# Attention's two ends reordered in a fused graph network kernel: V's products, VectorE's head sums, and Wo before the last centring

## The chip, the cores and the metric

One core of one Trainium2 chip. The metric is the device time of one execution in microseconds (us), the median of several runs. The kernel before took 464.77 us (three runs, 464.75 to 464.81).

## What is computed

The kernel fuses four graph-network layers on 512 nodes with 512 features, fp32. Only the first is touched, and in it only the attention. The softmax runs over axis 1 of scores with shape (node, head, other node), that is over the **heads**, not over the nodes:

```
q = (x @ Wq + bq).reshape(N, H, HEAD)        # N = 512, H = 8, HEAD = 64
k = (x @ Wk + bk).reshape(N, H, HEAD)
v = (x @ Wv + bv).reshape(N, H, HEAD)
scores = einsum('nhd,mhd->nhm', q, k) / sqrt(HEAD)
scores = where(adj[:, None, :] == 0, -1e9, scores)
attn = softmax(scores, axis=1)               # over the 8 heads
attn_out = einsum('nhm,mhd->nhd', attn, v).reshape(N, D) @ Wo + bo
h1 = layer_norm(x + attn_out, g1, be1)
ff = relu(h1 @ W1 + b1) @ W2 + b2
return layer_norm(h1 + ff, g2, be2)
```

The three later layers (a mean over edges, four experts over edges, a normalised graph convolution) follow one another and each needs the whole result of the one before.

## The kernel before, in words

**Engines and order.** Each engine has its own instruction list, written out by hand, and waits on semaphores; nothing is reordered at run time. TensorE is PE in the profile, VectorE DVE, ScalarE ACT, GpSimd POOL, and SyncE (SP) issues most DMAs.

**Tiling of the attention.** It runs in `STEPS = 8` steps. Step i takes a tile of 128 of the other nodes (m, `mt = i % 4`) and one half, 256, of the query nodes (`half = i // 4`), for all 8 heads. In each step:

- `scores(i, g)` for g = 0 and 1, four heads each: two bf16 matmuls that write the mask (L1415) and four score products (L1419, in the trace eight passes). The groups rotate through three pairs of PSUM banks, so a group from the third on waits until ACT has exponentiated the group two before it (`exp_done`).
- `coarse_scores(i, g)` on ACT copies the group's scores to bf16 (L655); a copy waits on `max_read`, VectorE's reading of the step before. `maxima(i)` on VectorE is the maximum over heads in three instructions (L923 or L928, L930, L933), the last of which writes `m_bf`.
- `centre(i, g)` on PE subtracts that maximum from the scores by two matmuls (L1426).
- `exponentials(i)` on ACT, two activations (L641), one a group.
- The sum over heads: GpSimd adds pairs of heads in two instructions (L537, `pair_sum`), then VectorE reduces these (L951, `head_sum`), except in step 0, where VectorE does it with four additions of its own (L943 to L948). `head_inverse` is a reciprocal (L957), and `normalised(i)` scales the exponentials (L399).
- `values(i, part_no)` on PE multiplies the probabilities by V (L1441, eight passes for four heads), and adds into banks 0 and 1. After steps 3 and 7 ACT copies these out (`attended_out`, L646), and `att_made` lets PE begin `values(4, 0)` and the Wo products.

**V.** V's tiles are four accumulating products each (L1331, two passes each in the trace), which PE works off in pieces (`values_part(t, *steps)`) between the scores of the first steps; VectorE adds the bias row (`values_in(t)`, L911). V products wait for all four tiles.

**After the steps** come the Wo tiles (`plain_rows_tile`, L1331), each followed on VectorE by residual, layer norm statistics and normalisation (`h1_start`, `h1_finish`), then transposes (L1282) and W1 (from L1509).

**GpSimd's other work nearby:** the last quarter of W1's low half (L490, waiting on `sums_made`), two DMAs that add rows to x_sb and h_sb, and the power for each layer norm (L505). SP's next weight load waits for that L490.

**VectorE's order around the change** (before):

```
head_sum(0); maxima(1); values_in(2); head_inverse(0); normalised(0)
maxima(2); head_sum(1); values_in(3); head_inverse(1)
for i in 2..7: maxima(i + 1); normalised(i - 1); head_sum(i); head_inverse(i)
```

Of the kernel before, what the change touches and what calls it, by code (L numbers as in the profile page):

```python
# [39 lines left out]
def build(nc, d, out):  # L40
    N, D = d["x"].shape
    E = d["src"].shape[0]
    NT = N // P
# [9 lines left out]
    STEPS = 2 * NT  # L53
# [196 lines left out]
    with ctx:  # L250
# [214 lines left out]
        def _(gp):  # L465
# [56 lines left out]
            gp.wait_ge(total_ask, 1)  # L522
            for k in range(DT - 1):
                split_lo_tile(W1A, k)
            gp.wait_ge(sums_made, 1)
            split_lo_tile(W1A, DT - 1)
            gp.wait_ge(ln_out, ln_out_no(LN0, NT - 1))
            add_row("L0_gnn_be2", x_sb, be2_added)
            gp.wait_ge(tr_done, tr_no(T0, NT - 1))
            add_row("L0_gnn_bo", h_sb, bo_added)  # L530
            for i in range(1, STEPS):

                e, pairs = e_bufs[i % E_BUFS], pair_sums[i % 2]
                gp.wait_ge(sums_made, max(i - 1, 1))
                for g in range(2):
                    gp.wait_ge(exp_done, 2 * i + g + 1)
                    gp.tensor_tensor(pairs[:, :, 2 * g:2 * g + 2].rearrange("p n h -> p h n"), e[:, 4 * g:4 * g + 2],  # L537
                                     e[:, 4 * g + 2:4 * g + 4], ALU.add).then_inc(pairs_made, 1)
# [26 lines left out]
        def _(act):  # L565
# [78 lines left out]
            def attended_out(half):  # L644
                act.wait_ge(pv_done, 2 * NT * (half + 1))
                nc.scalar.activation(att_sb[:, :, half * HN:(half + 1) * HN], attended(), ACT.Copy)\  # L646
                  .then_inc(att_made, 1)

            def coarse_scores(i, g):

                act.wait_ge(score_done, 2 * i + g + 1)
                if i >= 1:
                    act.wait_ge(max_read, i)
                heads = s_bf[:, g * HEADS // 2:(g + 1) * HEADS // 2]
                nc.scalar.activation(heads.rearrange("p (w b) n -> p w b n", w=2), group_scores(i, g), ACT.Copy)\  # L655
                  .then_inc(coarse_made, 1)

            coarse_scores(0, 0)
            for i in range(STEPS):
                exponentials(i)  # L660
                if i == 0:
                    coarse_scores(1, 0)
                if DIRECT <= i + 1 < STEPS:
                    coarse_scores(i + 1, 1)
                if i == NT + 2:
                    attended_out(0)
                if i + 2 < STEPS:
                    coarse_scores(i + 2, 0)
            attended_out(1)
# [90 lines left out]
        def _(v):  # L760
# [148 lines left out]
            def values_in(t):  # L909
                v.wait_ge(v_done, t + 1)  # L910
                nc.vector.tensor_tensor(v_sb[:, t, :], ps[:, v_bank(t), :], bv_row[:], ALU.add).then_inc(v_made, 1)  # L911
# [5 lines left out]
            def maxima(i):  # L917
                if i >= 1:
                    v.wait_ge(max_done, i)
                if i < DIRECT:  # L920
                    v.wait_ge(coarse_made, i + 1)
                    v.wait_ge(score_done, 2 * (i + 1))
                    nc.vector.tensor_tensor(s_max[:].rearrange("p (w b) n -> p w b n", w=2),  # L923
                                            s_bf[:, 0:4].rearrange("p (w b) n -> p w b n", w=2), group_scores(i, 1),
                                            ALU.max).then_inc(max_read, 1)
                else:
                    v.wait_ge(coarse_made, 2 * i)
                    nc.vector.tensor_tensor(s_max[:], s_bf[:, 0:4], s_bf[:, 4:8], ALU.max).then_inc(max_read, 1)  # L928
                v.wait_ge(max_read, i + 1)
                link(nc.vector.tensor_tensor(s_max[:, 0:2], s_max[:, 0:2], s_max[:, 2:4], ALU.max))  # L930
                if i >= 1:
                    v.wait_ge(centred, 2 * i)
                nc.vector.tensor_tensor(m_bf[:], s_max[:, 0], s_max[:, 1], ALU.max).then_inc(max_done, 1)  # L933
# [4 lines left out]
            def head_sum(i):  # L938

                e, r = e_bufs[i % E_BUFS], rsum[:, i % 2, :]  # L940
                if i == 0:
                    v.wait_ge(exp_done, 1)
                    nc.vector.tensor_tensor(half_sum[:, 0:2], e[:, 0:2], e[:, 2:4], ALU.add).then_inc(first_half, 1)  # L943
                    v.wait_ge(exp_done, 2)
                    link(nc.vector.tensor_tensor(half_sum[:, 2:4], e[:, 4:6], e[:, 6:8], ALU.add))
                    v.wait_ge(first_half, 1)
                    link(nc.vector.tensor_tensor(half_sum[:, 0:2], half_sum[:, 0:2], half_sum[:, 2:4], ALU.add))
                    nc.vector.tensor_tensor(r, half_sum[:, 0], half_sum[:, 1], ALU.add).then_inc(sums_made, 1)  # L948
                else:
                    v.wait_ge(pairs_made, 2 * i)  # L950
                    nc.vector.tensor_reduce(r, pair_sums[i % 2][:], AX_X, ALU.add).then_inc(sums_made, 1)  # L951

            def head_inverse(i):

                r = rsum[:, i % 2, :]
                v.wait_ge(sums_made, i + 1)
                nc.vector.reciprocal(r, r).then_inc(rinv_made, 1)  # L957

            def normalised(i):

                v.wait_ge(rinv_made, i + 1)
                if i < STEPS - 1:
                    probabilities(nc.vector, i, slice(0, HEADS)).then_inc(prob_done, 2)
                else:
                    probabilities(nc.vector, i, slice(0, HEADS // 2)).then_inc(prob_done, 1)
                    probabilities(nc.vector, i, slice(HEADS // 2, HEADS)).then_inc(prob_done, 1)

            head_sum(0)
            maxima(1)
            values_in(2)  # L970
            head_inverse(0)
            normalised(0)
            maxima(2)
            head_sum(1)
            values_in(3)
            head_inverse(1)
            for i in range(2, STEPS):
                if i + 1 < STEPS:
                    maxima(i + 1)
                normalised(i - 1)  # L980
                head_sum(i)
                head_inverse(i)
# [283 lines left out]
        def _(pe):  # L1266
# [61 lines left out]
            def plain_rows_tile(bank, t, src, w, done, steps=(0, 1, 2, 3)):  # L1328

                for k in steps:  # L1330
                    last = nc.tensor.matmul(ps[:, bank, :], src[:, k, col(t)], w[:, k, :], start=k == 0,  # L1331
                                            stop=k == DT - 1)
                if k == DT - 1:
                    last.then_inc(done, 1)

            def values_part(t, *steps):
                plain_rows_tile(v_bank(t), t, T_sb, w_v, v_done, steps)
# [92 lines left out]
            def values(i, part_no):  # L1430

                mt = i % NT
                if i == 0:
                    pe.wait_ge(v_made, NT)
                if i == NT:
                    pe.wait_ge(att_made, 1)
                pe.wait_ge(prob_done, 2 * i + part_no + 1)
                for h in range(4 * part_no, 4 * part_no + 4):
                    rows = slice(HD * (h % 2), HD * (h % 2 + 1))
                    goal = ps[rows, h // 4, (h // 2 % 2) * HN:(h // 2 % 2 + 1) * HN]  # L1440
                    last = nc.tensor.matmul(goal, v_sb[:, mt, h * HD:(h + 1) * HD], e_bufs[i % E_BUFS][:, h, :],  # L1441
                                            start=mt == 0 and h % 4 < 2, stop=mt == NT - 1 and h % 4 >= 2,
                                            skip_group_check=True)
                last.then_inc(pv_done, 1)
# [2 lines left out]
            scores(0, 1)  # L1447
            values_part(1, 3)
            values_part(2, 0, 1)
            for i in range(STEPS):  # L1450
                centre(i, 0)
                centre(i, 1)
                if i == 0:
                    scores(1, 0)
                if i == 1:
                    values_part(3, 1)
                if i >= 3:
                    values(i - 3, 0)
                if i + 1 < STEPS:
                    scores(i + 1, 1)  # L1460
                if i >= 3:
                    values(i - 3, 1)
                if i + 2 < STEPS:
                    scores(i + 2, 0)
                if i == 0:
                    values_part(2, 2, 3)
                    values_part(3, 0)
                if i == 1:
                    values_part(3, 2, 3)
            values(STEPS - 3, 0)  # L1470
            values(STEPS - 3, 1)
            pe.wait_ge(raw_in["o"], 16)
            plain_rows_tile(wo_bank(0), 0, att_sb, w_o, wo_done)
            plain_rows_tile(wo_bank(1), 1, att_sb, w_o, wo_done)
            values(STEPS - 2, 0)
            values(STEPS - 2, 1)
# [281 lines left out]
```

## Time and profile before

| | us |
|---|---|
| median of 3 runs | 464.77 |
| the profiled execution's own time | 464.84 |
| its span, first to last instruction | 463.0 |
| attention's steps in the trace | about 60.7 to 129.7 |
| TensorE busy | 447.6 (97%) |
| VectorE busy | 306.4 (66%) |
| ScalarE busy | 190.9 (41%) |
| GpSimd busy | 164.0 (35%) |

Times in the rows below are microseconds from the start of the span. A matmul row's length includes the drain of its last pass, so back-to-back groups are read by the distance of their starts. What stands in square brackets is the time the engine sat idle before the row, and which instruction released it. A row of busy time by stretch has: the stretch, its length, the busy us of PE, PEld, DVE, ACT and POOL (x instructions), PE's granted clock as a share of full speed, the DMA engines' share, GB/s.

### The profile page before, as it was taken

How to read it: one execution, taken by the hardware profiler on the slowest of the kernel's cores; microseconds unless marked ns; L12 is line 12 of the kernel's file. 1: busy time of each engine (PE TensorE's matmuls, PEld its weight loads, DVE VectorE, ACT ScalarE, POOL GpSimd, SP SyncE). 2: the span in 40 equal slices, each digit the busy share in tenths (PEclk: the TensorE clock that was granted, in tenths of full speed). 3: DMA queues.
4: the chain of work that ended last, by engine and by line, in shares of the span. 5: the costliest groups of instructions: out<-in, count | busy, mean ns of one | idle time of the engine just before them, and what ended most of it. 6: DMA issues, size and time to landing. Idle time of an engine off the chain costs nothing.

```text
span 463.0 us, 5935 instructions
## 1 busy us (share of the span) xinstructions
PE 447.6 (97%) x2108; PEld 327.9 (71%) x2108; DVE 306.4 (66%) x556; ACT 190.9 (41%) x266; POOL 164.0 (35%) x109
## 2 busy tenths in 40 slices
PE   7999999798999999899999999999999999999997
PEld 3456544343459888678878888888888888888766
DVE  5999868899987998943866747152353237133865
ACT  5898834665133430451622262234303431227240
POOL 5000037433213863363244444144324444344100
PEclk9999999999999999899999999999999999999999
DMA  8870006600000745244020232223221331020002
GB/s 281 174 286 1 1 2 153 119 1 0 1 0 2 169 150 181 38 107 154 1 92 0 92 105 83 85 91 115 91 92 49 108 139 71 21 91 1 0 1 91
DMA packets 24202, 37.48 MB, mean 81 GB/s; under 512 B 5744, under 2 KB 6256, under 8 KB 24176
## 3 DMA queue, kind: packets, MB, share of 16 engines
q1 hardware_dynamic: 21728, 32.80, 21.3%
q0 software_dynamic: 2160, 4.19, 5.1%
q8 instruction: 18, 0.29, 0.2%
q10 hardware_dynamic: 288, 0.13, 0.1%
q14 instruction: 8, 0.07, 0.0%
HBM read 36.07 MB, written 1.05 MB: 80 GB/s over the span
## 4 chain that ended last, share of the span: by engine, by line
PE 84%; DVE 11%; ACT 2%; issue 1%; DMA 1%; POOL 0%; DVEq 0%
PE ps L1269 17%; PE ps L1270 17%; PE ps L1271 17%; PE ps L1342 5%; PE ps L1331 5%; PE ps L1298 3%; PE ps L1297 3%; PE ps L1324 2%; DVE e_sb L399 2%; PE ps L1419 2%; PE ps L1441 2%; DVE rsum L957 1%; DVE stats L772 1%; PE ps L1282 1%; DVE rsum L951 1%
## 5 line engine op out<-in xcount | busy, mean ns | idle before, releaser
L481 POOL TENSOR_TENSOR w_lo<-w_stage,w_hi 128x1024 fp32r<-128x1024 f32 x21 | 52.0, 2476 | 134.0 <-ACT w_hi L569 124.2
L569 ACT ACTIVATE w_hi<-w_stage 128x2048 fp32r<-128x2048 f32 x22 | 42.0, 1909 | 53.4 <-PE ps L1271 53.4
L482 POOL TENSOR_TENSOR w_lo<-w_stage,w_hi 128x1024 fp32r<-128x1024 f32 x21 | 55.3, 2631 | 0.0
L1269 PE MATMUL ps<-w_hi,hid_hi 128*128 128x512 f32 x112 | 43.6, 389 | 0.0
L1270 PE MATMUL ps<-w_lo,hid_hi 128*128 128x512 f32 x112 | 43.6, 389 | 0.0
L1271 PE MATMUL ps<-w_hi,hid_lo 128*128 128x512 f32 x112 | 43.6, 389 | 0.0
L1269 PE MATMUL ps<-T_hi,w_hi 128*128 128x512 f32 (+1 forms) x108 | 39.3, 364 | 0.0
L505 POOL TENSOR_TENSOR rstd<-vareps,scalars 128x1 f32<-128x1 f32 x24 | 16.3, 680 | 63.1 <-DVE vareps L774 63.1
L1271 PE MATMUL ps<-T_hi,w_lo 128*128 128x512 f32 (+1 forms) x108 | 38.6, 358 | 0.0
L1270 PE MATMUL ps<-T_lo,w_hi 128*128 128x512 f32 (+1 forms) x108 | 38.6, 358 | 0.0
L1169 DVE TENSOR_SCALAR tmp<-ps,bl 128x512 f32<-128x512 f32 x16 | 12.0, 750 | 39.9 <-ACT hid_hi L723 39.9
L846 DVE TENSOR_SCALAR one_src<-iota_n,edge_m,edge_w 128x256 f16 x128 | 34.3, 351 | 0.4 <-POOL edge_w L520 0.4
L537 POOL TENSOR_TENSOR pair_sum<-e_sb 128x512 f32<-128x512 f32 x14 | 20.8, 1506 | 23.0 <-ACT e_sb L641 23.0
L574 ACT ACTIVATE h_sb<-x_sb,shift,rstd 128x512 f32<-128x512 f32 x16 | 13.0, 813 | 37.4 <-DVE shift L782 37.4
L1175 DVE TENSOR_TENSOR z_lo<-ps,z_hi 128x512 fp32r<-128x512 f32 x16 | 10.9, 692 | 25.4 <-ACT z_hi L728 25.4
L490 POOL TENSOR_TENSOR w_lo<-w_stage,w_hi 128x512 fp32r<-128x512 f32 x4 | 5.0, 1266 | 56.6 <-DVE checked L871 48.0
L1269 PE MATMUL ps<-agg_hi,w_hi 128*128 128x512 f32 x64 | 25.0, 391 | 0.0
L1271 PE MATMUL ps<-agg_hi,w_lo 128*128 128x512 f32 x64 | 24.9, 389 | 0.0
L1270 PE MATMUL ps<-agg_lo,w_hi 128*128 128x512 f32 x64 | 24.9, 389 | 0.0
L1297 PE MATMUL ps<-z_hi,c_hi 128*128 128x512 f32 x64 | 24.9, 389 | 0.0
L1298 PE MATMUL ps<-z_lo,c_hi 128*128 128x512 f32 x64 | 24.9, 389 | 0.0
L1270 PEld LDWEIGHTS ps<-w_lo,hid_hi 128*128 128x128 f32 x112 | 21.0, 188 | 4.4
(236 smaller groups left out, 1037.1 us busy)
## 6 DMA issues: line engine op xcount, KB each, us to landing
w_stage<-in_L_gnn_Wr SPq DMA_DIRECT2D x8, 1024.0 KB, 5.3
w_stage<-in_L_gnn_Wl SPq DMA_DIRECT2D x8, 1024.0 KB, 5.1
w_stage<-in_L_gnn_W SPq DMA_DIRECT2D x5, 1024.0 KB, 5.6
x_sb<-in_x SPq DMA_DIRECT2D x4, 256.0 KB, 3.5
w_q<-in_L_gnn_Wq SPq DMA_DIRECT2D x1, 1024.0 KB, 6.9
w_k<-in_L_gnn_Wk SPq DMA_DIRECT2D x1, 1024.0 KB, 9.5
w_v<-in_L_gnn_Wv SPq DMA_DIRECT2D x1, 1024.0 KB, 5.8
w_o<-in_L_gnn_Wo SPq DMA_DIRECT2D x1, 1024.0 KB, 11.1
```

The costliest lines, as they stand in the source:

```text
L481: gp.tensor_tensor(w_lo[h][:, 0:2], stage[s][:, 0:2], f32(w_hi[h][:, 0:2]), ALU.subtract)
L482: gp.tensor_tensor(w_lo[h][:, 2:4], stage[s][:, 2:4], f32(w_hi[h][:, 2:4]), ALU.subtract)\
L537: gp.tensor_tensor(pairs[:, :, 2 * g:2 * g + 2].rearrange("p n h -> p h n"), e[:, 4 * g:4 * g + 2], e[:, 4 * g + 2:4 * g + 4], ALU.add).th ...
L569: nc.scalar.activation(w_hi[home(u)][:], stage[u % 2][:], ACT.Copy).then_inc(hi_made, 1)
L846: last = nc.vector.tensor_scalar(one_src[:, bass.ds(slot, 1), :].squeeze(1), iota_n[:, 0:HALF], edge_m[:, 0, bass.ds(c, 1)], edge_w[:, bas ...
L1269: nc.tensor.matmul(goal, a_hi, b_hi, start=start, stop=False, **kw)
L1270: nc.tensor.matmul(goal, a_hi, b_lo, start=False, stop=False, **kw)
L1271: return nc.tensor.matmul(goal, a_lo, b_hi, start=False, stop=stop, **kw)
L1297: nc.tensor.matmul(goal, counts_hi[:, k, col(t)], r_hi[:, k, :], start=k == 0, stop=False)
L1298: return nc.tensor.matmul(goal, counts_hi[:, k, col(t)], r_lo[:, k, :], start=False, stop=k == NT - 1)
L1331: last = nc.tensor.matmul(ps[:, bank, :], src[:, k, col(t)], w[:, k, :], start=k == 0, stop=k == DT - 1)
L1342: last = nc.tensor.matmul(ps[:, bank, :], w[:, k, col(j)], T_sb[:, k, :], start=k == 0, stop=k == DT - 1)
```

## The change

On **PE**: of V's third tile only one part stays before `centre(1)`; the others, and the fourth tile, are spread singly over steps 1 and 2. From step 5 on the V products move forward: `values(3, 0)` stands at the end of step 5, before `centre(6)`, and `values(3, 1)` and `values(4, 0)` in step 6. New in front of `centre(7)` are the first two of the four products of Wo's first tile (`first_rows(0, 1)`, which waits for Wo's load and for 14 exponentials). The other two come after `values(4, 1)`.

On **VectorE**: step 1 also sums its heads alone, by four additions; `values_in(2)` and `values_in(3)` go later, and `head_inverse(0)` and `head_sum(1)` come before `maxima(2)`. On **GpSimd**: no pair sums in step 1, and the last quarter of W1's low half waits for VectorE's second maximum. On **ACT**: `attended_out(0)` stands before `coarse_scores(7, 1)`, not after it.

```diff
-            gp.wait_ge(sums_made, 1)
+            gp.wait_ge(max_done, 2)
             split_lo_tile(W1A, DT - 1)
...
-            for i in range(1, STEPS):
+            for i in range(2, STEPS):
                 e, pairs = e_bufs[i % E_BUFS], pair_sums[i % 2]
-                gp.wait_ge(sums_made, max(i - 1, 1))
+                gp.wait_ge(sums_made, i - 1)
...
                 exponentials(i)
                 if i == 0:
                     coarse_scores(1, 0)
+                if i == NT + 2:
+                    attended_out(0)
                 if DIRECT <= i + 1 < STEPS:
                     coarse_scores(i + 1, 1)
-                if i == NT + 2:
-                    attended_out(0)
...
             def head_sum(i):
-                if i == 0:
-                    v.wait_ge(exp_done, 1)
+                if i < 2:
+                    v.wait_ge(exp_done, 2 * i + 1)
...
             head_sum(0)
             maxima(1)
+            head_inverse(0)
+            head_sum(1)
+            maxima(2)
+            normalised(0)
+            head_inverse(1)
             values_in(2)
-            head_inverse(0)
-            normalised(0)
-            maxima(2)
-            head_sum(1)
-            values_in(3)
-            head_inverse(1)
             for i in range(2, STEPS):
                 if i + 1 < STEPS:
                     maxima(i + 1)
+                if i == 2:
+                    values_in(3)
                 normalised(i - 1)
...
+            def first_rows(*steps):
+                pe.wait_ge(raw_in["o"], 16)
+                pe.wait_ge(exp_done, 2 * STEPS - 2)
+                plain_rows_tile(wo_bank(0), 0, att_sb, w_o, wo_done, steps)
+
             for i in range(STEPS):
                 centre(i, 0)
                 centre(i, 1)
                 if i == 0:
                     scores(1, 0)
-                if i == 1:
+                elif i == 1:
+                    values_part(2, 3)
+                elif i == 2:
                     values_part(3, 1)
-                if i >= 3:
+                elif i < STEPS - 2:
                     values(i - 3, 0)
+                elif i == STEPS - 2:
+                    values(i - 3, 1)
                 if i + 1 < STEPS:
                     scores(i + 1, 1)
-                if i >= 3:
+                if i == 1:
+                    values_part(3, 0)
+                elif i == 2:
+                    values_part(3, 2, 3)
+                elif 3 <= i < STEPS - 2:
                     values(i - 3, 1)
+                elif i == STEPS - 2:
+                    values(i - 2, 0)
                 if i + 2 < STEPS:
                     scores(i + 2, 0)
                 if i == 0:
-                    values_part(2, 2, 3)
-                    values_part(3, 0)
-                if i == 1:
-                    values_part(3, 2, 3)
+                    values_part(2, 2)
+                elif i == STEPS - 3:
+                    values(i - 2, 0)
+                elif i == STEPS - 2:
+                    first_rows(0, 1)
+            values(STEPS - 4, 1)
+            first_rows(2, 3)
             values(STEPS - 3, 0)
             values(STEPS - 3, 1)
-            pe.wait_ge(raw_in["o"], 16)
-            plain_rows_tile(wo_bank(0), 0, att_sb, w_o, wo_done)
             plain_rows_tile(wo_bank(1), 1, att_sb, w_o, wo_done)
```

## Rows read from the trace of the kernel before

**Rows 1.** The page's chain of work that ended last, by engine.

```profile
PE 84%; DVE 11%; ACT 2%; issue 1%; DMA 1%; POOL 0%; DVEq 0%
```

**Rows 2.** Busy time by stretch: steps 4 to 6.

```profile
95.07:114.42 19.35, 17.21 (x110) 7.84 (x111) 19.04 (x19) 12.53 (x13) 7.75 (x6) 1.00 0.00 1
```

**Rows 3.** Timeline of PE, steps 0 to 2: start, us, instruction, [idle before].

```profile
72.27 2.84 PE L1331 MATMUL ps<-w_v,T_sb 128*128 128x512 f32 x6
74.95 1.03 PE L1426 MATMUL ps<-m_bf,neg_ident 128*128 128x512 bf16 x4
...
76.67 0.59 PE L1415 MATMUL ps<-no_edge,neg_ident 128*128 128x512 bf16 x2
...
78.26 0.61 PE L1415 MATMUL ps<-no_edge,neg_ident 128*128 128x512 bf16 x2
...
82.52 1.04 PE L1426 MATMUL ps<-m_bf,neg_ident 128*128 128x512 bf16 x4 [0.68 <-DVE m_bf L933]
```

**Rows 4.** Timeline of DVE, steps 0 to 2, and one steady step from 93.60.

```profile
68.30 0.69 DVE L943 TENSOR_TENSOR half_sum<-e_sb 128x512 f32<-128x512 f32 x1 [1.57 <-ACT e_sb L641]
...
71.01 1.21 DVE L923 TENSOR_TENSOR s_max<-s_bf,ps 128x1024 bf16<-128x1024 bf16 x1
...
72.75 0.29 DVE L933 TENSOR_TENSOR m_bf<-s_max 128x256 bf16<-128x256 bf16 x1
...
76.74 2.29 DVE L399 TENSOR_TENSOR e_sb<-e_sb,rsum 128x2048 f32<-128x2048 f32 x1
79.50 1.22 DVE L928 TENSOR_TENSOR s_max<-s_bf 128x1024 bf16<-128x1024 bf16 x1 [0.46 <-ACT s_bf L655]
80.75 1.38 DVE L930 TENSOR_TENSOR s_max<-s_max 128x512 bf16<-128x512 bf16 x1
...
83.51 0.68 DVE L911 TENSOR_TENSOR v_sb<-ps,row 128x512 f32<-128x512 f32 x1
...
93.60 0.63 DVE L928 TENSOR_TENSOR s_max<-s_bf 128x1024 bf16<-128x1024 bf16 x1
...
94.93 2.28 DVE L399 TENSOR_TENSOR e_sb<-e_sb,rsum 128x2048 f32<-128x2048 f32 x1
...
98.38 1.75 DVE L957 RECIPROCAL rsum<-rsum 128x256 f32<-128x256 f32 x1
```

**Rows 5.** Timeline of ACT (step 1) and of POOL (steps 1 and 4).

```profile
75.58 1.94 ACT L641 ACTIVATE e_sb<-ps 128x1024 f32<-128x1024 f32 x2 [2.17 <-PE ps L1426]
...
76.75 5.11 POOL L537 TENSOR_TENSOR pair_sum<-e_sb 128x512 f32<-128x512 f32 x2 [1.56 <-ACT e_sb L641]
...
97.02 2.59 POOL L537 TENSOR_TENSOR pair_sum<-e_sb 128x512 f32<-128x512 f32 x2 [3.87 <-ACT e_sb L641]
```

**Rows 6.** Timeline of PE from step 6 to the first transposes of h.

```profile
107.97 1.04 PE L1426 MATMUL ps<-m_bf,neg_ident 128*128 128x512 bf16 x4 [0.18 <-DVE m_bf L933]
...
114.42 1.04 PE L1426 MATMUL ps<-m_bf,neg_ident 128*128 128x512 bf16 x4 [1.78 <-DVE m_bf L933]
...
118.99 7.13 PE L1331 MATMUL ps<-w_o,att_sb 128*128 128x512 f32 x16
126.06 3.67 PE L1441 MATMUL ps<-e_sb,v_sb 128*64 128x256 f32 x32
...
134.39 1.04 PE L1282 MATMUL ps<-ident,h_sb 128*128 128x128 f32 x8
```

**Rows 7.** Timeline of ACT and DVE after the last step.

```profile
129.78 1.02 ACT L646 ACTIVATE att_sb<-ps 128x1024 f32<-128x1024 f32 x1 [12.71 <-PE ps L1441]
...
124.83 2.36 DVE L399 TENSOR_TENSOR e_sb<-e_sb,rsum 128x1024 f32<-128x1024 f32 x2
...
134.59 0.69 DVE L991 TENSOR_TENSOR h_sb<-ps,h_sb 128x512 f32<-128x512 f32 x1 [1.02 <-PE ps L1331]
```

**Rows 8.** After the feed-forward: PE's idle, and busy time with granted clock.

```profile
190.16 0.66 PE L1282 MATMUL ps<-ident,h_sb 128*128 128x128 f32 x4 [2.03 <-ACT h_sb L574]
...
192.00:194.00 2.00, 2.00 (x6) 1.55 (x5) 1.90 (x5) 0.00 (x0) 0.47 (x1) 0.50 0.20 36
```

More of the change, by code:

```diff
@@ L940, in head_sum @@
                 e, r = e_bufs[i % E_BUFS], rsum[:, i % 2, :]
-                if i == 0:
-                    v.wait_ge(exp_done, 1)
+                if i < 2:
+                    v.wait_ge(exp_done, 2 * i + 1)
                     nc.vector.tensor_tensor(half_sum[:, 0:2], e[:, 0:2], e[:, 2:4], ALU.add).then_inc(first_half, 1)
-                    v.wait_ge(exp_done, 2)
+                    v.wait_ge(exp_done, 2 * i + 2)
                     link(nc.vector.tensor_tensor(half_sum[:, 2:4], e[:, 4:6], e[:, 6:8], ALU.add))
-                    v.wait_ge(first_half, 1)
+                    v.wait_ge(first_half, i + 1)
                     link(nc.vector.tensor_tensor(half_sum[:, 0:2], half_sum[:, 0:2], half_sum[:, 2:4], ALU.add))
@@ L949, in head_sum @@
                 else:
-                    v.wait_ge(pairs_made, 2 * i)
+                    v.wait_ge(pairs_made, 2 * (i - 1))
                     nc.vector.tensor_reduce(r, pair_sums[i % 2][:], AX_X, ALU.add).then_inc(sums_made, 1)
```

## The prediction, made before the changed kernel ran

> **What bounds the kernel now.** First the chain that ended last: 84% of it is TensorE, 11% VectorE [rows 1]. TensorE is the bound, so a gain has to come where it waits, or where it follows another engine. Next the busy time by stretch: from centring 4 to centring 7 VectorE works 19.04 of 19.35 us and TensorE 17.21 [rows 2], so these three steps of 6.45 us are VectorE's. Then the two timelines around each centring. Centring 1 starts at 74.95 with no idle ahead of it, though its maximum was begun at 72.75: TensorE was still on three V parts begun at 72.27 [rows 3, 4]. Centring 2 has 0.68 us of idle in front [rows 3], because VectorE's maximum 2 ran from 79.50 to 82.38 (its first two instructions 1.22 and 1.38 us), where a steady step takes 93.60 to 94.93 [rows 4]. Centring 7 has 1.78 us of idle in front [rows 6]. After it TensorE has no gap to the Wo tiles: its 3.67 us of V products, 7.13 of Wo, 3.67 of V products [rows 6], while VectorE still finishes steps 6 and 7. So the change touches two pieces: the start, where TensorE delays VectorE and GpSimd collides with it, and the end, where TensorE's own sum of work counts. Between them VectorE sets the pace, and what it gains at the start is kept.
>
> **The start, step by step.** Unit prices: a V part is 0.89 us (2.84 for three, starts 0.445 a pass apart) [rows 3]; a group of scores 1.60 (76.67 to 78.26) [rows 3]; from the start of a group to the maximum that needs it 2.83 (76.67 to 79.50) [rows 3, 4]; centring to exponential 0.63 (74.95 to 75.58), two exponentials 1.94, exponential to pair sum 1.17 [rows 3, 5]. VectorE: own sums 2.71 (68.30 to 71.01), a maximum alone 1.33, V's bias 0.6 (lasting 0.68, less the overlap of neighbours), scaling and reduction together 3.45 (94.93 to 98.38), of which the scaling is 2.2; the reciprocal is what is left of 6.45 after 93.60 to 98.38, that is 1.67 [rows 4, 6].
>
> Centring 1 now waits for one V part, not three: 72.27 + 0.89 = 73.16, 1.79 earlier. The V parts moved are not saved, 2 x 0.89 here; they go behind centrings 1 and 2, where TensorE had gaps. Scores (2,1) stand behind centring 1 and one V part as before, so they start at about 74.91 and allow maximum 2 at 77.74. VectorE: maximum 1 is over at 72.96, reciprocal 0 until 74.63, first exponential of step 1 there at 73.79 + 1.06 = 74.85, own sums (the same four additions as in step 0, for one reduction of about 1.2) until 77.56. They lie beside the scores: maximum 2 starts at 77.74, not 79.50.
>
> Maximum 2 is then cheaper too. In the trace GpSimd's first pair sum starts at 76.75, 0.01 us behind the scaling at 76.74, and the two take 5.11 us where they take 2.59 in a steady step [rows 4, 5]; the maximum laid over them takes 2.88 instead of 1.33 to 1.39. The change takes GpSimd out of step 1. Maximum 2 ends at 79.1, and centring 2 starts at about 79.27, 3.25 earlier. The page "SBUF — State Buffer" of the Trainium skill (Who interferes with whom) says that VectorE with two SBUF inputs and a GpSimd instruction reading SBUF exclude one another for the whole instruction; the trace agrees (2.29 us of scaling and then the steady 2.59 of sums are 4.9 of the 5.11), and by it the moved sums cost no lock unless pair sums 2 reach maximum 3, which is a rival below.
>
> Then the engines come level. VectorE: scaling 0 until 81.3, reciprocal 1 until 83.0, V bias until 83.6. TensorE and ScalarE: scores (3,0) end at 74.91 + 1.60 + 0.89 + 1.60 = 79.0; ScalarE copies them (1.02) before it may exponentiate step 2, whose first half is there at 81.05; scores (3,1) start at 81.06 and allow maximum 3 at 83.89. That is the later one, so 83.89 counts. Pair sums 2: exponential 79.98, + 1.17 = 81.15, held by the scaling until about 81.35, + 2.5 = 83.85, just clear. Maximum 3, V bias (moved to here, in VectorE's way): 83.89 + 1.39 + 0.60 + 3.45 + 1.67 = **91.0** for maximum 4. Before it stood at 93.60 [rows 4]: **2.6 us gained**. TensorE needs for the same point: scores (3,1), two V parts, scores (4,0), centring 3 at 86.05; ScalarE's copy is in front of the exponential at 87.04; scores (4,1) at 88.12 allow 90.95. It reaches centring 4 at 92.36, and VectorE at 91.0 + 1.47. All three within 0.1 us: no slack. GpSimd's W1 quarter now starts 1.9 us later (72.96 instead of 71.1), and behind it on its queue the two adding DMAs and, by SP's wait, a weight load; the pair sums behind them start only at 81.15, and the readers of the data come after 127. I cost this at nothing; without that cover it is 1.9 us. If VectorE alone counted, maximum 4 would be at 90.5 (3.1 gained); with one more maximum under pair sums, 1.49 later (1.1 gained).
>
> **The end, on the old time axis** (subtract 2.6). Values (3,0) are one group of eight passes, 3.67 / 4 = 0.92, about 1.02 between other work. Step 5 has only 0.18 of idle [rows 6], so centring 6 is 0.84 late, at 108.81. Behind it values (3,1) and scores (7,1) as before, so maximum 7 could start at 109.95 + 0.84 + 2.83 = 113.63 (scores (7,1) stood 0.97 + 1.01 behind centring 6's 107.97). VectorE was ready at 112.95 (93.60 + 3 x 6.45): it loses **0.68**. ScalarE's copy of attention's first half, 1.02 (the same instruction as at 129.78) [rows 7], now stands ahead of the score copy: exponentials 6 from 109.44 to 111.3, copy to 112.3, score copy due at 112.5. Hidden by 0.2; uncovered it would cost up to 1.02. Values (4,0) need that copy too (112.4, when TensorE comes). Then the first two Wo products: four passes of 0.445 = 1.78, until 115.22, against maximum 7 at 115.1. Centring 7 at 115.22, 0.8 late, but the 1.78 of idle is filled, and 1.02 + 1.78 of work is behind it already.
>
> From centring 7: 0.97, three value groups 2.70, twelve Wo passes 5.35, some 0.15 for changes of kind, so values (6) begin at 124.4, not 126.06 [rows 6]. Now VectorE ends last: its halved scaling 7 begins at 124.83 + 0.68, halves done at 126.7 and 127.87. Values (7,1) start at 127.93, where before they did at 126.06 + 2.70 = 128.76: **0.83 earlier**. The copy-out moves from 129.78 to 128.95. Wo's third tile and transposes 0 follow it, 0.83 early. But transposes 1 wait for VectorE's second normalised tile. Before, VectorE was done with it at 134.59 - 1.02 = 133.57 [rows 7]; now at 134.25. TensorE takes 134.31 + 0.44 = 134.75, against 134.39 + 0.88 = 135.27 [rows 6]. So **0.5 us** stays of the end. Wo's fourth tile and all of W1 stand behind that on TensorE.
>
> **Sum.** 2.6 + 0.5 = 3.1 us. Profiled execution 464.84 - 3.1 = 461.7 (span 463.0 to 459.9; 1.84 lies around the span and stays). The profiled execution is 0.07 over the median, so median **461.7** as well, to a tenth.
>
> The rest of the kernel moves as a block. One place there could answer differently: TensorE is idle for 2.03 us before 190.16, and from 192 to 194 its granted clock is 0.50, the lower of its levels (1.2 against 2.4 GHz) [rows 8]. If moving by 3 us keeps the fall away there, little comes of it (under 0.2 us, since ScalarE's normalised rows are late there anyway); if it came to a packed stretch instead, the 2 us of the row alone would cost 1.0, and with its edges, which the row does not show, I take 1.6. The page "TensorE: Matmul & The Clock Gate" of the Trainium skill (What's actually happening) says the gate's window is free-running, which would allow both; no row here shows it.
>
> **Rivals.**
> 1. *The end pays nothing.* VectorE's delay is not 0.68 but the full 1.2 or more, because ScalarE's copy-out is not hidden by its 0.2 us. Then transposes 1 end where they did. For: VectorE decides the end from 0.52 further on. Against: it takes a copy that starts late or lasts over 1.2 us, and L646 has 1.02 [rows 7]. 461.7 + 0.5 = 462.2. Chance 0.14.
> 2. *Pair sums reach a maximum at the start.* Margins 0.04 us at maximum 3 and 0.2 at maximum 4 by my times. It costs 0.1 to 1.49 once: up to 463.2. That rule of the SBUF page is its mechanism. Chance 0.13.
> 3. *The clock falls in a packed stretch.* 463.3. Against: the clock is 1.00 in rows 2 with 2.1 us of idle spread over it, and the change removes idle. Chance 0.05.
> 4. *More than forecast*: VectorE alone sets the start, or TensorE's 0.83 comes through. 460.8 to 461.3. Chance 0.12.
> 5. *It does not do what it says*: centring 1 comes earlier, but a thing after the attention that does not depend on it (a weight load, an adding DMA) sets the end: 464.8. Against: TensorE is 84% of the chain, DMA 1% [rows 1]. Chance 0.03.
> 6. *Slower: locked collision.* The same meeting of pair sums and maximum, in each of steps 3 to 7, as levelled engines keep one phase. 5 x 1.49 = 7.5 lost: 469.1. It decides from three steps on (4.5 against 3.1). For: no slack at the start. Against: in a steady step pair sums end at 97.02 + 2.59 = 99.61 and the next maximum starts at 93.60 + 6.45 = 100.05, and a late one just moves along. Chance 0.03.
>
> **How the numbers follow.** Forecast 0.50, own range 461.3 to 462.1. The range for 8 in 10 takes in rivals 1, most of 2 and of 4, and not 3, 5, 6: 460.9 to 463.1. A measurement can tell about 0.2% (0.9 us) from no change, so the border is 463.8: faster 0.50 + 0.14 + 0.13 + 0.05 + 0.12 = 0.94; same 0.03; slower 0.03.
>
> **What would show it.** Right: centring 1 at about 73.2 with no idle; maximum 2 at 77.7 taking 1.35; maximum 4 at 91.0; centring 7 at 112.6 with under 0.3 idle in front; copy-out of the second half at 126.3; transposes 1 idle for about 0.5 before them, on VectorE. Wrong: a maximum's first instruction over 0.7 us; a score copy waiting behind the copy-out at step 6; an idle before centring 4 that names TensorE's own queue; the first W1 products not 3 us early.

## The result

The changed kernel takes 461.93 us (median of five, 461.69 to 462.57), the kernel before 464.75 on the same chip: 2.82 us less, ratio 0.9941 (95% interval 0.9931 to 0.9952). The forecast was 461.7. The profiled execution took 462.0 with a span of 460.2, against 464.84 and 463.0.

The page of the changed kernel: busy time by engine, and the chain that ended last.

```profile
PE 450.0 (98%) x2108; PEld 328.2 (71%) x2108; DVE 307.8 (67%) x559; ACT 190.8 (41%) x266; POOL 158.0 (34%) x107
...
PE 81%; DVE 12%; ACT 2%; issue 2%; DVEq 1%; DMA 1%; POOL 0%
```

GpSimd has lost two pair sums and about 6 us of busy time, VectorE has gained three instructions and 1.4 us. TensorE has the same 2108 instructions, and the shares of the chain that ended last are within 3 points of those in [rows 1], so the gain has to be read by place.

The changed kernel's timeline of PE, steps 0 to 4 (answers to [rows 3]):

```profile
72.33 1.13 PE L1332 MATMUL ps<-w_v,T_sb 128*128 128x512 f32 x2
73.30 1.03 PE L1427 MATMUL ps<-m_bf,neg_ident 128*128 128x512 bf16 x4
...
79.38 1.04 PE L1427 MATMUL ps<-m_bf,neg_ident 128*128 128x512 bf16 x4 [0.16 <-DVE m_bf L933]
80.26 1.02 PE L1332 MATMUL ps<-w_v,T_sb 128*128 128x512 f32 x2
81.27 0.61 PE L1416 MATMUL ps<-no_edge,neg_ident 128*128 128x512 bf16 x2
...
92.77 1.04 PE L1427 MATMUL ps<-m_bf,neg_ident 128*128 128x512 bf16 x4
```

Centring 1 moved from 74.95 to 73.30, centring 2 from 82.52 to 79.38. The timeline of DVE for the same stretch and for step 6 (answers to [rows 4]):

```profile
74.98 0.69 DVE L943 TENSOR_TENSOR half_sum<-e_sb 128x512 f32<-128x512 f32 x1 [0.25 <-ACT e_sb L641]
...
77.85 0.69 DVE L928 TENSOR_TENSOR s_max<-s_bf 128x1024 bf16<-128x1024 bf16 x1
78.58 0.42 DVE L930 TENSOR_TENSOR s_max<-s_max 128x512 bf16<-128x512 bf16 x1
...
84.11 0.69 DVE L928 TENSOR_TENSOR s_max<-s_bf 128x1024 bf16<-128x1024 bf16 x1 [0.38 <-ACT s_bf L655]
...
91.23 0.69 DVE L928 TENSOR_TENSOR s_max<-s_bf 128x1024 bf16<-128x1024 bf16 x1
...
97.75 0.63 DVE L928 TENSOR_TENSOR s_max<-s_bf 128x1024 bf16<-128x1024 bf16 x1
...
111.26 0.69 DVE L928 TENSOR_TENSOR s_max<-s_bf 128x1024 bf16<-128x1024 bf16 x1 [0.54 <-ACT s_bf L655]
```

Maximum 2 takes 0.69 and 0.42 where it took 1.22 and 1.38. Maximum 4 stands at 91.23, forecast 91.0, before 93.60. Maximum 5 is at 97.75, against 100.05 one period after 93.60: the start gave 2.30 us. At maximum 7 VectorE sits idle for 0.54, which the kernel before did not have.

The timeline of PE and ACT at the end (answers to [rows 6, 7]):

```profile
111.06 1.98 PE L1332 MATMUL ps<-w_o,att_sb 128*128 128x512 f32 x4
112.88 1.03 PE L1427 MATMUL ps<-m_bf,neg_ident 128*128 128x512 bf16 x4
...
122.27 1.95 PE L1442 MATMUL ps<-e_sb,v_sb 128*64 128x256 f32 x16
124.57 2.13 PE L1442 MATMUL ps<-e_sb,v_sb 128*64 128x256 f32 x16 [0.35 <-DVE e_sb L399]
...
131.36 1.29 PE L1283 MATMUL ps<-ident,h_sb 128*128 128x128 f32 x8
132.49 1.04 PE L1499 MATMUL ps<-ident,ct_hi 128*128 128x128 f32 x8
...
126.75 1.02 ACT L646 ACTIVATE att_sb<-ps 128x1024 f32<-128x1024 f32 x1 [11.24 <-PE ps L1442]
```

The 1.78 us of idle in front of centring 7 are gone, the last V products wait 0.35 for VectorE, and the transposes of h take 1.13 (131.36 to 132.49) where 0.87 is the plain length: 0.26 us of waiting for VectorE's second tile lie inside the group. They end 2.78 us before their old 135.27. With 2.30 from the start, the end gave 0.48. The first W1 product stands at 136.40 where it stood at 139.17, 2.77 earlier.

### The profile page after: what moved, and what is told of

The parts are those of the page before. It is cut to its first block, busy times and chain, and to the rows that moved or that the text cites. A ratio compares the mean times of both kernels' runs of the same rounds, so it can differ in the third digit from the quotient of the medians.

```text
span 460.2 us, 5938 instructions
## 1 busy us (share of the span) xinstructions
PE 450.0 (98%) x2108; PEld 328.2 (71%) x2108; DVE 307.8 (67%) x559; ACT 190.8 (41%) x266; POOL 158.0 (34%) x107
## 4 chain that ended last, share of the span: by engine, by line
PE 81%; DVE 12%; ACT 2%; issue 2%; DVEq 1%; DMA 1%; POOL 0%
PE ps L1270 17%; PE ps L1272 17%; PE ps L1271 17%; PE ps L1343 4%; PE ps L1299 3%; PE ps L1298 3%; PE ps L1332 3%; DVE e_sb L399 2%; PE ps L1420 2%; PE ps L1325 2%; DVE rsum L957 1%; PE ps L1442 1%; DVE one_src L846 1%; DVE stats L772 1%; PE ps L1283 1%
## 5 line engine op out<-in xcount | busy, mean ns | idle before, releaser
L1270 PEld LDWEIGHTS ps<-w_hi,hid_hi 128*128 128x128 f32 x112 | 21.0, 188 | 4.4
```

The costliest lines, as they stand in the source:

```text
L1270: nc.tensor.matmul(goal, a_hi, b_hi, start=start, stop=False, **kw)
```

## The experiments

All medians are of five or more executions, each beside executions of the kernel before on the same chip (median 464.72 in the first four, 464.80 and 464.79 later). The gain is against that; the changed kernel's is 2.82. Diffs are against the changed kernel unless it is said otherwise; `...` marks what is left out.

**Start alone.** The end as in the kernel before; on ScalarE (not shown) the copy-out stands behind the score copy again:

```diff
                 elif i == 2:
                     values_part(3, 1)
-                elif i < STEPS - 2:
+                else:
                     values(i - 3, 0)
-                elif i == STEPS - 2:
-                    values(i - 3, 1)
...
-                elif i == STEPS - 3:
-                    values(i - 2, 0)
-                elif i == STEPS - 2:
-                    first_rows(0, 1)
-            values(STEPS - 4, 1)
-            first_rows(2, 3)
             values(STEPS - 3, 0)
             values(STEPS - 3, 1)
+            pe.wait_ge(raw_in["o"], 16)
+            plain_rows_tile(wo_bank(0), 0, att_sb, w_o, wo_done)
```

> The changed kernel with its end undone (V products, Wo's first tile and the copy-out of attention as in the kernel before); the start as changed. Theory (start and end add up, the start carries most): maximum 4 stands 2.4 us before its old place and all of it reaches the end of the kernel, 464.75 - 2.4 = 462.35; centring 7 has its 1.8 us of idle in front again. Rival A (the end pays nothing): the same time as the changed kernel, 461.9. Rival B (the end carries more than I think, because VectorE's loss at step 6 is only a shift): 462.8 or more.

Measured: 462.39, against 464.72, ratio 0.9949 (0.9936 to 0.9963): 2.33 us. Centring 7 has its idle again:

```profile
112.03 1.04 PE L1427 MATMUL ps<-m_bf,neg_ident 128*128 128x512 bf16 x4 [1.78 <-DVE m_bf L933]
```

All that VectorE gains at the start arrives at the end of the kernel, as the theory had it; rival A (461.9) and rival B (462.8) lie outside the range of its executions, 462.22 to 462.54.

**End alone.** The kernel before with the changed end (the same lines the other way round, V's parts and VectorE's order untouched).

> The kernel before with the end of the change alone: V products from step 5 on moved ahead, two Wo products in front of the last centring, ScalarE's copy-out ahead of the score copy. Theory: 464.75 - 0.4 = 464.35; centring 6 is 0.7 late, VectorE loses 0.6 at maximum 7, TensorE has no idle in front of centring 7 and 0.35 in front of the last V products. Rival A: the delay at step 6 eats everything, 464.75 or slower. Rival B: TensorE's filled idle comes through, 463.9.

Measured: 464.35 (464.17 to 465.09), ratio 0.9993 (0.9984 to 1.0002). The interval takes in no change, so the size of 0.37 us rests on the trace. There the three marks that the theory named stand as forecast: VectorE's idle at maximum 7, no idle in front of centring 7, and 0.35 before the last V products.

```profile
113.70 0.69 DVE L928 TENSOR_TENSOR s_max<-s_bf 128x1024 bf16<-128x1024 bf16 x1 [0.53 <-ACT s_bf L655]
...
115.32 1.03 PE L1426 MATMUL ps<-m_bf,neg_ident 128*128 128x512 bf16 x4
...
127.01 2.13 PE L1441 MATMUL ps<-e_sb,v_sb 128*64 128x256 f32 x16 [0.35 <-DVE e_sb L399]
```

Start and end add up, within what the executions spread: 2.33 + 0.37 = 2.70 of 2.82.

**Step 1's head sums back to GpSimd**, V's parts and the end as changed. With the sums two things go back that hang on them: scaling 0 stands ahead of maximum 2, and W1's last quarter waits for the first head sum:

```diff
-            gp.wait_ge(max_done, 2)
+            gp.wait_ge(sums_made, 1)
...
-                if i < 2:
+                if i < 1:
...
             head_inverse(0)
-            head_sum(1)
-            maxima(2)
             normalised(0)
+            maxima(2)
+            head_sum(1)
             head_inverse(1)
```

> The changed kernel with only the head sums of step 1 given back to GpSimd (VectorE: reciprocal 0, scaling 0, maximum 2, reduction 1, reciprocal 1, V bias 2). V's parts spread as changed. Theory (port held in turn): GpSimd's sums wait for scaling 0 (about 74.7 to 76.9) and then lie over maximum 2, which takes 2.2 us or more in place of 1.39; centring 2 about 0.9 late, maximum 4 about 0.85 late: 462.8. Rival A (spreading V carries the start alone, the sums' place does not matter): 461.9. Rival B (the reduction being 1.5 us shorter than own sums pays): under 461.7.

Measured: 463.01 (462.90 to 463.24), a gain of 1.71, 1.1 less than the changed kernel's. Timeline of POOL and DVE:

```profile
75.21 4.89 POOL L537 TENSOR_TENSOR pair_sum<-e_sb 128x512 f32<-128x512 f32 x2
...
74.98 2.29 DVE L399 TENSOR_TENSOR e_sb<-e_sb,rsum 128x2048 f32<-128x2048 f32 x1
77.96 1.00 DVE L928 TENSOR_TENSOR s_max<-s_bf 128x1024 bf16<-128x1024 bf16 x1 [0.68 <-ACT s_bf L655]
79.00 1.38 DVE L930 TENSOR_TENSOR s_max<-s_max 128x512 bf16<-128x512 bf16 x1
```

The scaling started 0.23 us earlier than the sums and had its usual 2.29; the sums had to wait for it and took 4.89. Then they in turn held up maximum 2: 77.96 to the reduction at 80.61, 2.65 us for 1.39. The second pair sum took 1.72 in its turn, where one takes 1.28 alone. So the taking turns is shown in both directions, as the Trainium skill has it ("SBUF — State Buffer", Who interferes with whom: whoever issues first gets the pair for the whole instruction); the trace agrees. VectorE's own sums cost it 1.5 us more instructions than the reduction, and with scaling 0 behind maximum 2 they are still worth 1.1 us. W1's quarter ran at 71.34 here and at 73.15 in the changed kernel; it did not delay the pair sums, which start 1.18 us behind their exponential here and 1.17 in step 2 of the changed kernel.

**V's parts back together**, own sums kept:

```diff
                 elif i == 1:
-                    values_part(2, 3)
-                elif i == 2:
                     values_part(3, 1)
...
                 if i == 0:
-                    values_part(2, 2)
+                    values_part(2, 2, 3)
+                    values_part(3, 0)
+                elif i == 1:
+                    values_part(3, 2, 3)
```

> The changed kernel with only V's parts put back where they were (three in front of centring 1, one in front of scores (2,1), two behind scores (3,0)). Own sums kept. Theory: centring 1 is 1.66 late, scores (2,1) and maximum 2 1.7 late, TensorE comes late to centring 2 as well, about 81.7, and maximum 4 about 2.2 late: 464.1. Rival A (GpSimd's absence is the larger half): maximum 4 only 1 us late, 462.9. Rival B: V's placement does not matter, 461.9.

Measured: 463.99 (463.81 to 464.21), a gain of 0.73, 2.1 less than the changed kernel's. In its trace of PE centring 1 is at 75.06, and centring 2, at 81.79, has no idle before it: TensorE is late, not the maximum, whose last instruction ends at 81.09.

```profile
79.97 1.98 PE L1332 MATMUL ps<-w_v,T_sb 128*128 128x512 f32 x4
81.79 1.03 PE L1427 MATMUL ps<-m_bf,neg_ident 128*128 128x512 bf16 x4
```

Taken out one at a time, the two halves of the start cost 1.1 and 2.1 us, together more than the 2.3 they bring: they are not a sum but two conditions. Each maximum waits for the later of TensorE's scores and VectorE's queue.

**ScalarE's copy-out behind the score copy**, as before the change:

```diff
-                if i == NT + 2:
-                    attended_out(0)
                 if DIRECT <= i + 1 < STEPS:
                     coarse_scores(i + 1, 1)
+                if i == NT + 2:
+                    attended_out(0)
```

> The changed kernel with one order put back on ScalarE: the copy-out of attention's first half behind the score copy of step 7, as before. Theory: values (4,0) then wait for a copy-out that ends at about 112.1 and not 110.0, so TensorE idles 2 us in step 6, centring 7 comes 2 us late (114.9), of which the 0.35 us that TensorE waits for VectorE in front of the last V products take a part: about 1.5 us over the changed kernel, 463.4. Rival A: no difference, 461.9, since the 0.2 us that hide the copy are not needed. Rival B: faster (461.7), because the score copy no longer risks standing behind it.

Measured: median 464.29 of eleven, but these fall into two groups, five at 463.22 to 463.52 and six at 464.29 to 464.68; the mean granted clock was 0.996 in the first and 0.993 to 0.995 in the others. The first group (463.37 on average, 1.4 over the changed kernel) is about the 1.5 us that the theory gave: TensorE idles 2.04 us for the copy-out, and centring 7 starts at 114.87. The 1.2 us between the groups nobody had forecast, and the next two runs are on them.

**The same kernel again, for the trace of a longer execution.**

> The kernel f_copy_later once more, to see a profile of its longer executions: eleven had given 463.2 to 463.5 at a mean granted clock of 0.996 (five) and 464.3 to 464.7 at 0.993 to 0.995 (six). Theory: the 1.2 us between them are a second fall of the granted clock, in the packed stretch behind TensorE's 2.0 us of idle in step 6; a profile of a longer execution then shows a clock of 0.5 somewhere in 113 to 120, and Wo or V passes of about 0.43 us distance there. Rival: the fall after 188 lasts twice as long, and the stretch after step 6 stays at 1.00.

Measured: eight executions with a median of 464.00, and the same two groups: four at 462.98 to 463.28 (clock 0.996), four at 464.73 to 464.83 (0.993), and the profiled one is of the longer. Its timeline of PE, and busy time by stretch (the third column from the right is the granted clock):

```profile
112.09 1.08 PE L1442 MATMUL ps<-e_sb,v_sb 128*64 128x256 f32 x8 [2.04 <-ACT att_sb L646]
113.11 3.68 PE L1332 MATMUL ps<-w_o,att_sb 128*128 128x512 f32 x4
116.61 1.04 PE L1427 MATMUL ps<-m_bf,neg_ident 128*128 128x512 bf16 x4
```

```profile
108.00:112.00 4.00, 2.06 (x16) 0.80 (x10) 3.40 (x4) 2.94 (x4) 2.52 (x2) 1.00 0.00 0
112.00:114.00 2.00, 1.91 (x9) 0.91 (x10) 1.97 (x3) 0.04 (x1) 0.00 (x0) 0.80 0.00 0
114.00:116.00 2.00, 2.00 (x4) 0.83 (x3) 2.00 (x2) 0.00 (x0) 0.00 (x0) 0.50 0.00 0
```

The same stretch in the shorter execution's trace, from the run before:

```profile
112.00:116.00 4.00, 3.97 (x18) 1.73 (x20) 3.94 (x4) 0.44 (x1) 0.00 (x0) 1.00 0.00 0
```

After 2.04 us of idle the clock fell to 1.2 GHz, and the four Wo passes that take 1.82 us in the changed kernel (111.06 to 112.88) took 3.50 (113.11 to 116.61). The fall past the feed-forward is in both traces and about as long (between 188 and 196), so the rival is out. Of the 1.7 us lost there 1.2 (first run's groups) to 1.6 (second's) arrive at the end, 1.5 between the two spans, 462.9 and 461.4; a part was slack against VectorE at the transposes of h (the group lasts 1.07 us in the shorter execution's trace, 0.88 here).

**Blank matmuls in that wait** (against the kernel just shown):

```diff
                 elif i == STEPS - 2:
+                    pe.wait_ge(exp_done, 2 * STEPS - 2)
+                    blank(8)
                     values(i - 2, 0)
```

> f_copy_later with eight blank matmuls (zeros, 128x512 f16, 0.22 us each) in TensorE's wait in front of values (4,0), written to a bank that is free there; they add nothing to the result. Theory (the idle in step 6 lets the clock fall): the idle shrinks from 2.0 to 0.2 us, no second fall is granted, all executions lie at 463.2 to 463.5, median 463.4. Rival (the longer executions have another cause): the two groups stay, median between 463.4 and 464.6.

Measured: 463.18 (463.10 to 463.46, five executions), none in the longer group. Had each of them the chance of the two runs before (10 of 19 longer), five short ones would come 2 times in 100 (9/19 five times over). The idle in front of the V products is down to 0.20 us there, and the granted clock is 1.00 from 112 to 116. So the idle lets the clock fall, and filling it with useless work prevents that.

**V products ahead, Wo's first tile whole behind centring 7.**

```diff
                 elif i == STEPS - 3:
                     values(i - 2, 0)
-                elif i == STEPS - 2:
-                    first_rows(0, 1)
             values(STEPS - 4, 1)
-            first_rows(2, 3)
+            first_rows(0, 1, 2, 3)
```

> The changed kernel with all four products of Wo's first tile behind values (4,1); the V products stay moved ahead. Theory: TensorE idles 1.7 us in front of centring 7 and has that much more to do after it; values (7) come 1.2 us later, against slack of 0.35: 0.9 us over the changed kernel, 462.8. So the Wo products carry the end, and V products alone moved ahead lose 0.4 against the start alone (462.4). Rival: the V products' move carries the end and Wo's place does not matter, 461.9.

Measured: 462.53 (462.46 to 462.65), a gain of 2.27, so 0.55 less than the changed kernel's and level with the start alone (2.33). The theory's direction, but 0.35 less than its size: centring 7 comes at 112.80 with 1.67 of idle, the copy-out of the second half at 127.64 instead of 126.75. That is 0.89, as forecast; yet 0.26 of it was waiting at the transposes that then falls away.

**V products as before, the first two Wo products in front of centring 7.** ScalarE's copy-out stands behind the score copy again (not shown).

```diff
-                elif i < STEPS - 2:
+                else:
                     values(i - 3, 0)
...
-                elif i == STEPS - 3:
-                    values(i - 2, 0)
                 elif i == STEPS - 2:
+                    pe.wait_ge(att_made, 1)
                     first_rows(0, 1)
-            values(STEPS - 4, 1)
             first_rows(2, 3)
```

> The changed kernel with the V products back in their old steps, so that centring 6 is on time; the first two Wo products still in front of centring 7, where they wait for ScalarE's copy-out, which stands behind the score copy as before. Theory: VectorE loses nothing at maximum 7 (start 0.63 after the previous reciprocal, no idle), TensorE idles 1.1 us and then works 1.8, centring 7 is 1.1 late, and the end comes out level with the changed kernel's: 461.95. The 0.6 us that VectorE loses in the changed kernel and the work that the V products' move brings forward pay for each other. Rival A: VectorE's loss is the costly one, 461.5. Rival B: the late centring 7 is, 462.4.

Measured: 462.25 (462.00 to 462.50), a gain of 2.55: 0.2 more than the start alone, 0.3 less than the changed kernel, and so nearer to rival B than to the theory, though its executions lie among the changed kernel's. VectorE is on time (maximum 7 at 110.81 without idle), TensorE idles 1.12 us before the Wo products. What was missed is the price of the splitting. From the first Wo product to the last V products:

```profile
111.62 1.99 PE L1332 MATMUL ps<-w_o,att_sb 128*128 128x512 f32 x4 [1.12 <-ACT att_sb L646]
113.44 1.03 PE L1427 MATMUL ps<-m_bf,neg_ident 128*128 128x512 bf16 x4
114.40 1.95 PE L1442 MATMUL ps<-e_sb,v_sb 128*64 128x256 f32 x16
116.28 1.98 PE L1332 MATMUL ps<-w_o,att_sb 128*128 128x512 f32 x4
...
123.70 3.67 PE L1442 MATMUL ps<-e_sb,v_sb 128*64 128x256 f32 x32
```

That is 12.08 us for work that takes 11.63 unsplit (112.03 to 123.66 in the start alone). There are three more changes from one kind of matmul to another, so about 0.15 each, taken from one pair of traces. It accounts for the gain: against the start alone centring 7 is 1.16 later (1.12 + 1.82 - 1.78) with 1.82 of work ahead of it, which would be worth 0.66; less 0.45 that is 0.21, and 0.2 was measured.

**One count group into what idle is left** (against the last kernel). Of the four groups of transposes of the edge counts, one goes in front of the Wo products, to the free bank 7; two stand behind the last V products, one behind the transposes of h. ScalarE copies the early one out behind the last exponentials, and Wo's second tile waits for that copy (not shown):

```diff
                 elif i == STEPS - 2:
+                    pe.wait_ge(exp_done, 2 * STEPS - 2)
+                    count_transposes(ct_hi, 7, C_ROWS[0], c_tr)
                     pe.wait_ge(att_made, 1)
                     first_rows(0, 1)
```

> As e_rows_only, and one of the four groups of count transposes (0.44 us of TensorE) moved from after the second normalised tile to the idle in front of the Wo products, into a free pair of banks; ScalarE copies it out behind the last exponentials. Theory (TensorE's sum of work after centring 7 is what counts, as long as VectorE's chain is clear by more): 0.43 under e_rows_only, 461.5. Rival: VectorE's normalised tiles already set the end, then no difference to e_rows_only, 461.95.

Measured: 461.74 (461.61 to 461.92), ratio to before 0.9935 (0.9921 to 0.9948): 0.5 under the last kernel, as the theory said. TensorE's sum of work decides there, and VectorE has 0.57 us of idle at its third tile. Its gain of 3.06 is 0.24 more than the changed kernel's (461.93), and the executions of the two overlap, so no more than level with it can be claimed.

## Why the prediction held, point by point

- **Centring 1** at 73.30, forecast 73.2, with no idle. Right; of the 0.14 more, 0.06 were there before it (own sums of step 0 begin at 68.36, not 68.30), the rest is the V part, 0.97 from start to start and not 0.89.
- **Maximum 2** at 77.85 (77.74) in 1.39 us. Right, and the cause given is shown by the kernel with GpSimd's sums.
- **Maximum 4** at 91.23, forecast 91.0. The path was as forecast and its terms were a little short. By the forecast's sum maximum 3 hangs on TensorE's and ScalarE's side (VectorE has 0.38 of idle before it), so each tenth there counts. It came at 84.11 and not at 83.89. Of these 0.22, 0.17 were there when scores (3,0) began (77.57, forecast 77.40): the trace's 0.06, and two V parts behind scores at 0.97 and 0.96 from start to start instead of 0.89, less 0.03. Scores (3,1) then waited for ScalarE's exponential, as forecast, until 81.27 (forecast 81.06):

```profile
80.19 1.94 ACT L641 ACTIVATE e_sb<-ps 128x1024 f32<-128x1024 f32 x2
81.27 0.11 PEld L1416 LDWEIGHTS ps<-no_edge,neg_ident 128*128 128x128 bf16 x2 [0.82 <-ACT e_sb L641]
```

  The V part in front of them is therefore no price: it stands 1.01 before them (80.26 to 81.27), but 0.85 in the kernel with GpSimd's sums (81.63 to 82.48), where the exponential was in time. From maximum 3 to 4 it took 7.12, forecast 7.11. Centring 4 (92.77) waited for VectorE, 0.35 behind the start of its last instruction (92.42) as in the kernel before (94.72 to 95.07), with TensorE free at about 92.6; the forecast had the same order, 92.47 against 92.36. Maximum 4's first instruction took 0.69 where it had taken 0.63, which brings the 2.37 gained at its start to the 2.30 at maximum 5, in place of 2.6.
- **Pair sums and maximum 3** were to pass each other by 0.04 us. GpSimd's two took 2.55 from 81.36, so until 83.91, and maximum 3 began at 84.11, untouched: rival 2 did not come. A margin of 0.04 by times that missed by 0.2 was luck as much as reckoning. Rival 6 fell with it, since no maximum of steps 3 to 7 took more than 0.69 in its first instruction.
- **The end.** VectorE lost 0.61 at maximum 7 (111.26 against 112.95 - 2.30), forecast 0.68; centring 7 at 112.88 had no idle in front, forecast 112.6; 0.48 stayed, forecast 0.5. That is closer than its terms: the second copy-out is at 126.75, forecast 126.3, so TensorE came 0.73 earlier there than the start alone gives (129.78 - 126.75 - 2.30) and not 0.83, and the wait for VectorE at the transposes then took 0.26 of it. From centring 7 to values (6) it took 9.39 (112.88 to 122.27) where the forecast has 9.17: the 0.15 for changes of kind was too small by 0.22. That did no harm, since the V products behind still had to wait 0.35 for VectorE. That ScalarE's copy-out would be just hidden was right (it ends at 109.99, and the score copy starts at 110.13, behind scores that end at 110.08); moving it back cost 1.4 us, or 2.8 where the clock fell.
- **The sum** was 3.1, it is 2.8; the range 460.9 to 463.1 held.
- **The clock** (rival 3). The fall after the 2.03 us of idle past the feed-forward stayed and did little, as forecast: of the 51 executions of the kernel before beside these runs, the 25 at a mean clock of 0.996 averaged 464.83 and the 18 at 1.00 averaged 464.78. In the changed kernel's trace it is there too, and earlier, like the stretch around it:

```profile
188.00:190.00 2.00, 1.90 (x6) 1.49 (x6) 1.93 (x4) 0.60 (x1) 0.12 (x1) 0.53 0.78 131
```

  That a fall in a packed stretch would cost 1.6 was right in size, as the kernel with the later copy-out shows (1.68 on the four Wo passes). The changed kernel has no idle over 0.2 us between centrings 2 and 7, and none of its five executions has a mean clock under 0.996.

Not run alone were the later places of V's bias rows on VectorE and of W1's quarter on GpSimd; what each of them costs or brings is not shown.

## What to carry to other kernels

When two engines hand work to each other step by step, only the later one counts at each hand-over, so look for the steps where the wrong one is late; here one misplaced bundle of independent matmuls and one meeting on a shared port cost 2.3 us, which the steady steps behind them then carried to the end. A reordering on the bounding engine is to be priced with its changes from one kind of matmul to another (about 0.15 us each here), not only with its instructions. And a wait of 2 us on TensorE has two prices: its length, and now and then the clock.

## What the runs showed of the hardware

- After a wait of 2.04 us TensorE's granted clock fell to 1.2 GHz in a traced execution, and by their times and mean clocks in 10 of 19; in front of centring 7 the kernel before waits 1.78 us, and in its 51 executions beside these runs its mean clock was never under 0.996. With eight blank matmuls in the wait, no execution was of the longer kind.
- That program therefore has not one time but two, about 463.3 and 464.7, and a median of five would have been either. The page "TensorE: Matmul & The Clock Gate" of the Trainium skill (What's actually happening) says that the gate's window is free-running; that the same wait meets the fall in one execution and not in the next agrees with it.
- GpSimd's pair sums and VectorE's two-input instructions take turns, each holding the other up: 4.89 us for two sums that take 2.55 alone, 2.65 us for a maximum of 1.39.
